# Sandwich layer: the normalised residual turned by DMA as two fp16 planes instead of by TensorE, and the later steps re-spaced

## What is computed

```python
# attention, one head of width 256; the middle 128 input columns are multiplied in f32, the outer ones in fp16
q, k, v = split(mix_precision_matmul(x, weight_qkv), 3)
s = softmax(q / sqrt(256) @ k.T)
y = (s @ v) @ out_w.T + out_b

# feed-forward with a mix of each row and the row before it (zeros ahead of row 0 of a batch)
xr = mu_r * x + (1 - mu_r) * x_prev
xk = mu_k * x + (1 - mu_k) * x_prev
out = sigmoid(xr @ W_r.T) * (square(relu(xk @ W_k.T)) @ W_v.T)
```

## Time and profile before

| | |
|---|---|
| median of 3 runs | 842.78 us (842.33 to 846.61) |
| the profiled execution | 843.48 us |
| its span, first to last instruction | 841.7 us |
| mean granted TensorE clock | 0.975 |
| busy: PE, DVE, ACT, POOL | 797.7, 671.4, 514.2, 436.3 us |
| DMA queue of SP | 336496 packets, 100.56 MB, 57.3% of 16 engines |

### The profile page before, as it was taken

One profiled execution on the slowest core, in us unless ns is written; L12 is line 12 of the kernel. 1 busy time (PEld: TensorE's weight loads), 2 busy tenths in 40 slices (PEclk: granted clock), 3 DMA queues, 4 the chain that ended last, 5 costly groups with the idle time before them and its releaser, 6 DMA issues.

```text
span 841.7 us, 16181 instructions
## 1 busy us (share of the span) xinstructions
PE 797.7 (95%) x5873; PEld 582.9 (69%) x5873; DVE 671.4 (80%) x1805; ACT 514.2 (61%) x639; POOL 436.3 (52%) x654
## 2 busy tenths in 40 slices
PE   4888999999999999999999999999999999999953
PEld 3435777777777777777777777777777777778842
DVE  5698887888788888997788889887777788777673
ACT  3375656666567756666766656676665565665542
POOL 2110234665465556655545565556455654558862
PEclk8899999999999999999999999999999999999977
DMA  7565676666545687765456774846446555359100
GB/s 181 113 150 107 139 157 132 113 145 129 135 100 114 120 169 135 137 125 124 110 114 119 151 171 88 180 96 88 107 109 127 126 125 125 83 90 200 45 25 26
DMA packets 336575, 101.59 MB, mean 121 GB/s; under 512 B 310256, under 2 KB 336240, under 8 KB 336496
## 3 DMA queue, kind: packets, MB, share of 16 engines
q1 hardware_dynamic: 336496, 100.56, 57.3%
HBM read 18.75 MB, written 8.39 MB: 32 GB/s over the span
## 4 chain that ended last, share of the span: by engine, by line
PE 85%; DVE 9%; issue 2%; POOL 1%; ACT 1%; DMA 1%; SPq 0%; ACTq 0%; POOLq 0%; DVEq 0%
PE S L1047 6%; PE M L1015 6%; PE S L1048 6%; PE S L1051 6%; PE S L1049 6%; PE S L1050 6%; PE Y L1068 6%; PE Y L1072 6%; PE Y L1071 6%; PE Y L1070 6%; PE M L1017 6%; PE Y L1069 6%; PE M L1016 6%; PE M L1099 2%; DVE p_lo L823 1%
## 5 line engine op out<-in xcount | busy, mean ns | idle before, releaser
L807 DVE TENSOR_SCALAR_CACHE_REDUCE probs<-S 128x512 f32<-128x512 f32 x256 | 173.3, 678 | 98.4 <-PE S L1051 98.3
L609 ACT ACTIVATE probs<-probs,exp_bias,kappa 128x2048 f32<-128x2048 f32 x64 | 134.0, 2094 | 152.9 <-DVE exp_bias L818 152.9
L823 DVE TENSOR_TENSOR p_lo<-probs,p_hi 128x2048 f16<-128x2048 f32 x64 | 149.8, 2341 | 2.0 <-ACT p_hi L559 2.0
L507 POOL TENSOR_TENSOR xm_lo<-mixed,xm_hi 128x512 f16<-128x512 f32 x62 | 125.7, 2046 | 29.1 <-ACT xm_hi L559 29.1
L1072 PE MATMUL Y<-pt_hi,planes 128*128 128x256 f16 x512 | 139.8, 273 | 0.0
L1070 PE MATMUL Y<-pt_hi,planes 128*128 128x256 f16 x512 | 139.8, 273 | 0.0
L1069 PE MATMUL Y<-pt_lo,planes 128*128 128x256 f16 x512 | 139.8, 273 | 0.0
L1071 PE MATMUL Y<-pt_lo,planes 128*128 128x256 f16 x512 | 139.8, 273 | 0.0
L1068 PE MATMUL Y<-pt_hi,planes 128*128 128x256 f16 x512 | 139.8, 273 | 0.0
L559 ACT ACTIVATE p_hi<-probs 128x2048 f16<-128x2048 f32 x64 | 121.4, 1896 | 2.6 <-DMA pt_lo<-p_lo 2.5
L512 POOL TENSOR_TENSOR sq_lo<-square,sq_hi 128x512 f16<-128x512 f32 x31 | 43.2, 1392 | 144.6 <-ACT sq_hi L661 144.6
(11 more groups left out here) (180 smaller groups left out, 1882.4 us busy)
## 6 DMA issues: line engine op xcount, KB each, us to landing
x_res<-in_L_attn_x SPq DMA_DIRECT2D x32, 256.0 KB, 3.5
out_x<-gate SPq DMA_DIRECT2D x32, 256.0 KB, 2.8
xs<-in_L_attn_x SPq DMA_DIRECT2D x28, 128.0 KB, 2.9
xs<-in_L_attn_x SPq DMA_DIRECT2D x14, 256.0 KB, 3.3
pt_hi<-p_hi SPq DMA_TRANSPOSE x64, 4.6
pt_lo<-p_lo SPq DMA_TRANSPOSE x64, 4.0
pt_hi<-in_L_attn_weight_qkv SPq DMA_DIRECT2D x3, 128.0 KB, 2.6
pt_hi<-in_L_attn_weight_qkv SPq DMA_DIRECT2D x1, 256.0 KB, 2.8
```

The source lines that it names most:

```text
L807: dve.tensor_scalar(probs[:, h % 2, t, c * BLK:(c + 1) * BLK], S[k % RING][:, :], 1.0, None, ALU.mult, ALU.max, accum_out=chunk_max[:, t, ...
L823: dve.tensor_tensor(p_lo[:, t, :], probs[:, h % 2, t, :], p_hi[:, t, :], ALU.subtract).then_inc(p_lo_made, 1)
```

## The change

For blocks 0 to 30 the turn of the normalised residual leaves PE. ACT makes a high fp16 plane of it (`mix_high`), POOL the low one (`mix_low`), one DMA transpose on SP's queue turns both (`turn_mix`, ahead of the probabilities' turn in the same slot), and POOL adds the turned planes to `xt` (`mix_in_sum`). The scale that ACT applied is folded into the reciprocal deviation of the residual (`mix_shrink`). Block 31 keeps the transposes on PE. The offsets of all steps from the difference on are set anew, most of them three to six slots later, and the two mixes and the two splits get slots of their own; receptance and keys stand in slots 53 and 54 instead of both in 50, the gate in 60 instead of 55, its statistics in 61, rsqrt and normalisation in 62. The copy of the queries' high plane moves by one slot. PE no longer waits for `xt_made` before the queries.

```diff
@@ offsets
     MIX_IN = 39
+    MIX_HIGH = 40
+    MIX_LOW = 41
+    TURN_MIX = 42
     TURN = 41
     XT = 41
-    DIFF = 41
-    MIX = (44, 45)
-    SPLIT = 47
-    SPLIT_LOW = 47
-    RECEPT = 50
-    KEYS = 50
-    RECEPT_OUT = 53
-    SQUARE = 52
-    SQUARE_LOW = 52
-    FEED = 55
-    GATE = 55
-    GATE_STATS = 56
-    GATE_RSQRT = 56
-    GATE_NORM = 57
-    FINISH = 58
-    STORE = 63
+    DIFF = 45
+    MIX = (48, 50)
+    SPLIT = (49, 51)
+    SPLIT_LOW = (50, 52)
+    RECEPT = 53
+    KEYS = 54
+    RECEPT_OUT = 54
+    SQUARE = 55
+    SQUARE_LOW = 56
+    FEED = 58
+    GATE = 60
+    GATE_STATS = 61
+    GATE_RSQRT = 62
+    GATE_NORM = 62
+    FINISH = 63
+    STORE = 65
     QUERY = -6
-    Q_HIGH = -6
+    Q_HIGH = -5
@@ SP
+            def turn_mix(h):
+                if h >= 1:
+                    sp.wait_ge(xt_made, h)
+                sp.wait_ge(mix_hi_made, h + 1)
+                sp.wait_ge(mix_lo_made, h + 1)
+                sp.dma_start_transpose(mxt.rearrange("p l t e r -> p (l t e) r"),
+                                       mx.rearrange("p l t e d -> p (l t e d)")).then_inc(mix_in, 16)
...
             for k in range(SLOTS):
+                if (h := at(k, TURN_MIX)) is not None and h < DRAIN:
+                    turn_mix(h)
                 for t in range(RT):
                     if (h := at(k, TURN_P[t])) is not None:
                         turn_probs(h, t)
@@ POOL
-                pool.tensor_tensor(rvar[:, :], rmv[:, :, 1], eps[:, :], ALU.add).then_inc(r_eps_added, 1)
+                if h == 0:
+                    pool.wait_ge(scales_made, 3 + RT)
+                pool.tensor_scalar(rvar[:, :], rmv[:, :, 1], EPS, mix_shrink[:, 1:2], ALU.add, ALU.mult).then_inc(r_eps_added, 1)
...
+            def mix_low(h):
+                if h >= 1:
+                    pool.wait_ge(mix_in, 16 * h)
+                pool.wait_ge(mix_hi_made, h + 1)
+                pool.tensor_tensor(mx[:, 1], att[:, h % 2].rearrange("p t (e d) -> p t e d", e=HALVES), mx[:, 0],
+                                   ALU.subtract).then_inc(mix_lo_made, 1)
+
+            def mix_in_sum(h):
+                pool.wait_ge(mix_in, 16 * (h + 1))
+                if h >= 2:
+                    pool.wait_ge(mixed_made, (h - 1) * 4)
+                    pool.wait_ge(carried, h)
+                pool.tensor_tensor(xt[:, h % 2, :, 1:ROWS + 1].rearrange("p e (t r) -> p t e r", t=RT), mxt[:, 0], mxt[:, 1],
+                                   ALU.add).then_inc(xt_made, 1)
...
+                if (h := at(k, MIX_LOW)) is not None and h < DRAIN:
+                    mix_low(h)
                 if (h := at(k, DIFF)) is not None:
                     if h < DRAIN:
+                        mix_in_sum(h)
                         differences(h)
                     carry(h)
@@ ACT
+            def mix_high(h):
+                act.wait_ge(mix_in_made, (h + 1) * RT)
+                if h >= 1:
+                    act.wait_ge(mix_in, 16 * h)
+                copy(mx[:, 0], att[:, h % 2].rearrange("p t (e d) -> p t e d", e=HALVES)).then_inc(mix_hi_made, 1)
...
-            def split_high(h):
+            def split_high(h, i):
                 if h >= 1:
                     act.wait_ge(key_done, h)
-                for i in range(2):
-                    act.wait_ge(mixed_made, h * 4 + 2 * i + 2)
-                    copy(xm_hi[:, i], mixed[:, i]).then_inc(xm_hi_made, 1)
+                act.wait_ge(mixed_made, h * 4 + 2 * i + 2)
+                copy(xm_hi[:, i], mixed[:, i]).then_inc(xm_hi_made, 1)
@@ PE
-                if (h := at(k, TURN)) is not None:
-                    turn_mix_in(h, k)
+                if (h := at(k, TURN)) is not None and h >= DRAIN:
+                    turn_mix_in(h)
...
                     pe.wait_ge(q_lo_made, h)
-                    if (turned_before := begun(k, TURN)) > 0:
-                        pe.wait_ge(xt_made, turned_before)
                     queries(h)
```

More of the change, by code:

```diff
@@ L544, in _ @@
                     add_attention(h)
+                if (h := at(k, MIX_LOW)) is not None and h < DRAIN:
+                    mix_low(h)
                 if (h := at(k, DIFF)) is not None:
                     if h < DRAIN:
+                        mix_in_sum(h)
                         differences(h)
                     carry(h)
-                if (h := at(k, SPLIT_LOW)) is not None and h < DRAIN:
-                    split_low(h)
+                for i in range(2):
+                    if (h := at(k, SPLIT_LOW[i])) is not None and h < DRAIN:
+                        split_low(h, i)
                 if (n := prep(k, PREP_RSQRT)) is not None:
@@ L628, in attention_norm @@
                                    scale=arstd[:, t:t + 1]).then_inc(att_normed, 1)
[L630 to L640 removed]
+            def mix_high(h):
[3 more added lines that the diff above has]
+                copy(mx[:, 0], att[:, h % 2].rearrange("p t (e d) -> p t e d", e=HALVES)).then_inc(mix_hi_made, 1)
+            def mix_in_out(h):
+                act.wait_ge(mix_in_turned, 1)
+                act.wait_ge(mixed_made, (h - 1) * 4)
+                act.wait_ge(carried, h)
+                copy(xt[:, h % 2, :, 1:ROWS + 1], pair(TURN_BANK[:, :])).then_inc(xt_made, 1)
+            def split_high(h, i):
                 if h >= 1:
                     act.wait_ge(key_done, h)
[L643 to L645 removed]
+                act.wait_ge(mixed_made, h * 4 + 2 * i + 2)
+                copy(xm_hi[:, i], mixed[:, i]).then_inc(xm_hi_made, 1)
             def receptance(h):
@@ L689, in _ @@
                     attention_norm(h)
-                if (h := at(k, XT)) is not None:
+                if (h := at(k, MIX_HIGH)) is not None and h < DRAIN:
+                    mix_high(h)
+                if (h := at(k, XT)) is not None and h >= DRAIN:
                     mix_in_out(h)
@@ L695, in _ @@
                     squares(h)
-                if (h := at(k, SPLIT)) is not None:
-                    split_high(h)
+                for i in range(2):
+                    if (h := at(k, SPLIT[i])) is not None:
+                        split_high(h, i)
                 if (h := at(k, Q_HIGH)) is not None and h >= 1:
@@ L905, in differences, with split_low @@
                 dve.wait_ge(carried, h + 1)
+                dve.wait_ge(mixed_made, h * 4)
                 dve.tensor_tensor(diff[:, :, :], xt[:, h % 2, :, 1:ROWS + 1], xt[:, h % 2, :, 0:ROWS],
                                    ALU.subtract).then_inc(diff_made, 1)
-            def split_low(h):
-                for i in range(2):
-                    dve.wait_ge(xm_hi_made, h * 2 + i + 1)
-                    dve.tensor_tensor(xm_lo[:, i], mixed[:, i], xm_hi[:, i], ALU.subtract).then_inc(xm_lo_made, 1)
+            def split_low(h, i):
+                dve.wait_ge(xm_hi_made, h * 2 + i + 1)
+                dve.tensor_tensor(xm_lo[:, i], mixed[:, i], xm_hi[:, i], ALU.subtract).then_inc(xm_lo_made, 1)
             def squares_low(h):
@@ L970, in _ @@
                     differences(h)
-                if (h := at(k, SPLIT_LOW)) is not None and h >= DRAIN:
-                    split_low(h)
+                for i in range(2):
+                    if (h := at(k, SPLIT_LOW[i])) is not None and h >= DRAIN:
+                        split_low(h, i)
                 if (h := at(k, SQUARE_LOW)) is not None and h >= DRAIN:
```

32 lines of the change are left out of this document (14 added, 18 removed).

## The result

The changed kernel takes 853.42 us (median of 4 runs, 851.29 to 854.71) against 843.03 us (4 runs of the kernel before beside them): a ratio of 1.0121, 95% interval 1.0103 to 1.0140. It is slower by some 10 us, outside my range of 833 to 846. The execution profiled took 853.94 us, its span is 851.8.

What follows compares the result with a forecast made beforehand. It took a full PE to bound the kernel up to 758.39 us, and the order of small steps on four engines after 788.74; -13.1 + 9.4 = -3.7 us gave 839.0 us, range 833 to 846.

Steps and rivals of the forecast that it cites:

- The turn's price: PE-full stretch: four f32 transposes cost PE 0.44 us per row block; removing 29 such turns gains 12.7 us.
- I price the stall at 0: Receptance in the PE-full stretch: PE won't wait for the gate; 0 us, other bound 0.4 per period.
- preparation enters after gate and statistics and is absorbed by DVE's wait in slot 1: PE-full stretch: preparation of new rows on DVE fits in its wait for the projection, adding nothing.
- the margin: PE-full stretch: gate ready before PE reaches receptance at 16.73 us, by 0.75 us, 0.5 after p_lo's delay.
- Rival C: PE-full stretch: POOL's operations hold p_lo, the gate becomes PE's wait; 0.4 us per period gives +10, 849 us; 15%.
- The middle: Before the projection of block 30: PE waits 2.0 us instead of 1.1, from 1.3 and 0.7.
- The end: From the projection of block 30 to the end: later slots lengthen it from 52.96 to 62.4 us, by 9.4.
- Rival B: Cheap end: y_hi of 31 is not held, gate 29 doesn't hold the difference of 31; 833.5 us; 25%.
- Rival D: Late DMA: the mix turn delays the probabilities, up to 1 us for each of two blocks; 841 to 843 us; 10%.
- Rival E: The four transposes cost PE no time of their own, so 12.7 us are not gained; 852 us; 5%.
- the sum: Whole kernel: 13.1 us gained up to the projection of block 30, 9.4 lost after it, -3.7 in all.

Runs made afterwards that it cites:

- run 5: Changed kernel's new slots alone: the four f32 turns stay on PE, their copy on ACT, no planes, no DMA turn, nothing new on POOL; 855.88 us, ratio 1.0158.
- run 6: Changed kernel with its two added POOL operations cut to 4 of every 128 columns, leaving out that arithmetic; 842.51 us, ratio 0.9995 to the kernel before.
- run 2: Changed kernel with the reciprocals of the row sums three slots later on DVE (18 to 21); 846.04 us, ratio 1.0046 to the kernel before.
- run 8: Changed kernel, reciprocals at slot 21, block 27 in slots between, blocks 28 to 31 on old slots, turn on PE from 27; 848.20 us, ratio 1.0067.
- run 9: Changed kernel, reciprocals at 21, plans meeting at block 24: later blocks on old slots, reciprocals at 18, turn on PE from 24; 835.22 us, ratio 0.9924.
- run 10: Changed kernel, reciprocals at 21, plans meeting at block 26: later blocks on old slots, reciprocals at 18, turn on PE from 26; 846.63 us, ratio 1.0056.

## Why the prediction was wrong

**The turn's price: right.** Where nothing waits, a period is 23.70 us, and four L1099 are left. The DMA turn lands in 3.3 us and issues in 1.23 (3.5 and 1.6 were predicted); SP's later queue costs nothing in the stretch.

**The step that failed: "I price the stall at 0", and in it "preparation enters after gate and statistics and is absorbed by DVE's wait in slot 1".** Where there is no preparation, the working holds: in block 9 DVE takes up attention at 5.92 (predicted 5.9), the fourth score at 11.51 (11.5), p_lo ends at 14.95 (14.75), and the gate is there at 16.23 (15.96), 0.5 us before PE would need it at 16.73, and 0.5 was the margin. Two errors are hidden in it, and a pause of DVE covers both. The reciprocals were priced as in the kernel before, but the scaling takes 1.08 us in place of 0.23, and the earlier mixes 1.78 a pair; POOL's effect was looked for in p_lo alone. With preparation the pauses are gone: in block 11 the gate begins at 17.03 and PE starts the receptance at 17.85 in place of 16.73. The cost is 9.04 us in 13 periods where 0 was predicted.

Rival C named the wait and gave +10 for it, with a chance of 15%. That its sum is so near is partly luck: it had 0.4 us in each of 25 periods, and it was 0.1 to 1.3 in 13 and nothing in the others. Its reason was too simple as well: I blamed two more operations on POOL. Runs 5 and 6 show that the new slots alone cost 3.7 and that little POOL work in the new order costs 2.2, though the scaling is stretched to 920 ns in both; so its place beside the low split is not enough to bring about the 9.0. Run 2 shows that taking it away is enough to remove them: with it moved and all POOL work in place the excess is 0.9. POOL's sum was mis-sized too, 1.04 us predicted and 1.88 in the mean measured, and POOL was busy for 17.7 and 19.4 us in the two periods shown, where 16 to 17 were predicted.

**The middle: too small.** Between the old 753 and the projection of 30, waits of 1.3 us for y_lo at the projection of 29 and 0.7 for the probabilities of 31 and y_lo were predicted. Behind the last score tile PE waits 3.23 for y_lo at that projection (769.95), not at all for the second, and 1.17 for xm_lo at 759.48, which no term held: 4.4 in place of 2.0. The cause of the long one was right (y_hi held on ACT by a gate's normalisation); what made it so long stands on POOL, again a small step behind a large one of DVE (p_lo began at 764.13):

```profile
764.22 2.26 POOL L489 TENSOR_TENSOR gvar<-gmv,gate_eps 128x2 f32<-128x2 f32 x1
```

It took 0.20 in the kernel before. With the restarts of PE and a granted clock of 0.96 in place of 1.00 the piece from the last score tile to the projection of 30 is 3.9 us longer than predicted. So this projection is issued at 786.90, 1.8 us earlier than before, where 13.1 was predicted.

**The end: right in its steps, 2.5 us short.** Counted from that point, predicted and measured: y_lo of 31, for which its projection waits, 13.4 and the projection's first matmul 13.5; receptance 29 22.8 and 23.2; sq_lo of 30 41.4 and its feed begun at 43.2; relu 31 48.7 and 52.2; end 62.4 and 64.9. PE waits for y_lo and for the gate where it was said. I took the lower clock for one feed; it was granted over most of the end, 0.69 in the mean against 0.80, and behind the wait of 3.98 us at 800.44 the matmuls of projection 31 show 0.42 us each, at a granted clock of 0.50.

Of the 14.6 us that the end (from the last score tile) grew by, run 5 gives 9.3 to the slots, runs 5 and 6 give 0.9 to the DMA turn with ACT's copy and the narrow POOL work, less the four turns that leave PE there (100.57 less 99.71), and run 6 gives 4.5 to the full POOL work (105.03 less 100.57). These are differences between single profiles. Rival B fell with this. Rivals D and E fell too: no wait on the turned probabilities appears in the changed kernel, and PE's 0.43 us per period were real.

The 13.8 us missing in the sum are thus: 9.0 excess, 3.9 in the middle, 2.5 in the end, less 1.7 at the start that no term of the sum held (3.9 us ahead at block 7, where two turns and the feed that moves behind this point make 2.2).

**What stays open.** Why the first score tile of block 7 comes at 146.3 to 149.7 us in the profiles of runs 2, 8, 9 and 10, which are one and the same kernel up to there, so that 3.4 us of difference lie ahead of what was changed; the 1.7 us at the start may be of this kind. Which of POOL's two added operations does the greater harm. And how much of run 2's gain is the contention and how much the 0.34 us of work taken from in front of the gate.

## What to carry to other kernels

A margin that is built from the durations of the kernel before holds only as long as the same operations stand beside each other. When the order changes, look at every operation of DVE that will lie beside one of POOL, the tiny ones first: 0.23 became 1.08 us. Then build the margin for the fullest period, not for the usual one: here the usual one kept its 0.5 us, and the ones with extra work lost up to 1.3. A distance in slots is worth what fills the slots: later slots that cost the stretch little cost the end 9.3 us, and of three places for the change to the tighter plan only the one at which score tiles still filled the slots paid (835.2 us at block 24, 846.6 at 26). And a full engine does not show how close its suppliers are: one number moved cost the kernel before 6 us, and gained the changed one 7.

## What the runs showed of the hardware

- The same operation on 128x2 elements takes 0.23 us alone on DVE and 1.08 where a 128x512 subtraction of POOL started 0.1 us ahead of it; it ended where that one did (257.69 and 257.66). On POOL, the gate's shift of 128x2 went from 203 to 1864 ns in the mean when it came to begin just behind p_lo. The Trainium skill, SBUF — State Buffer, § Who interferes with whom, has the two engines exclude each other for a whole instruction when DVE's has two SBUF inputs and GpSimd's reads SBUF, or when DVE's is in a mode that takes both ports. The shift behind p_lo, which has two SBUF inputs, agrees; the scaling's times agree too, but by which of the two conditions it was held no run here tells. What I drew from it in the prediction was a delay of large operations; the small ones lose more, in proportion and here in sum (21.9 us of DVE's time for the scaling, 16.0 for the mixes).
- The granted clock of the end differs from run to run: 0.80 before, 0.69 in the changed kernel. Over the last 48 matmul instructions, in the same order of steps and behind the same idle time of 3.35 us, it was 0.73 before (first matmul 0.28 us) and 0.58 in run 9 (0.40), and the piece took 19.47 and 21.73 us; in run 10 it was 0.81 and 19.22 us. Whether that belongs to the kernel or to the one execution that was profiled is not shown: of 13 executions of the kernel before, one with a mean clock of 0.985 has a span of 839.9 us and the one with the lowest, 0.970, of 845.0.
- A sum of fp16 planes on POOL takes 1.15 us for 128x512 where nothing is beside it. For 128x16 it takes 0.22 in the median, and still 1.0 in the mean in the middle of DVE's work.
